# Payload and attribute rows in DRAM: from 16 and 132 bytes to 64 and 192 bytes

## The reference, cut to what matters

```python
def reference(x, src, dst, edge_attr_32, ...):
    edge_index = jnp.stack([src, dst])
    x = x + gnn(layernorm(x), edge_index, edge_attr_32, ...)     # relu(edge_attr @ W_time.T + b) summed over src
    x = x + moe6(layernorm(x), ...)                              # 6 experts of 3 layers, top 2
    x = x + gat2(layernorm(x), ..., src, dst)                    # 2 layers of graph attention, 256 channels
    x = x + routed_ffn(layernorm(x), ..., L1_ffn_edge_index)     # attention router over 131072 edges, 4 experts, top 2
    return x
```

## Time and profile before

| | |
|---|---|
| median of 3 runs | 10564.56 us (10502.92 to 10571.19) |
| the profiled execution | 10526.4 us |
| its span | 10524.6 us |
| TensorE's mean granted clock | 0.78 |
| busy: TensorE, VectorE, ScalarE, GpSimd | 53%, 52%, 34%, 55% |

### The profile page before, as it was taken

The page is one execution under the profiler, slowest core; times in us unless marked ns, Lnnn a source line. Parts: engine busy times, 40 slices in busy tenths (PEclk is TensorE's granted clock), DMA queues, the critical chain, the costliest instruction groups (busy, mean ns, idle before and its releaser), DMA issues. The chain is left out here.

```text
span 10524.6 us, 116781 instructions
## 1 busy us (share of the span) xinstructions
PE 5617.6 (53%) x22610; PEld 3283.4 (31%) x22610; DVE 5440.6 (52%) x18917; ACT 3525.9 (34%) x11436; POOL 5786.7 (55%) x5781
## 2 busy tenths in 40 slices
PE   0000001683321149936777764777772388888887
PEld 0000000571110025523444432444441134444444
DVE  8577300572200012235666654666664187777787
ACT  0000000230100012214555542555551076666662
POOL 3788767216577730045665654666666565565660
PEclk9999999995555579967777776777776577776678
DMA  4111100110000000003333321333330111111113
GB/s 126 24 21 22 24 9 4 27 33 2 2 23 1 1 1 0 0 22 85 88 86 85 87 63 55 86 86 87 88 87 15 23 20 23 22 23 23 23 23 99
DMA packets 476242, 426.24 MB, mean 40 GB/s; under 512 B 269726, under 2 KB 409876, under 8 KB 475668
## 3 DMA queue, kind: packets, MB, share of 16 engines
q0 software_dynamic: 214016, 282.62, 11.5%
q1 hardware_dynamic: 224020, 120.13, 4.2%
q10 hardware_dynamic: 37632, 17.48, 0.7%
HBM read 341.50 MB, written 78.72 MB: 40 GB/s over the span
## 5 line engine op out<-in xcount | busy, mean ns | idle before, releaser
L449 POOL DMA_INDIRECT pay_sorted<-pay,pos x1856 | 1880.9, 1013 | 1941.2 <-PEq L1217 762.7
L790 POOL DMA_INDIRECT G<-tab_gat,pay x1856 | 1783.6, 961 | 1314.1 <-issue 438.0
L790 POOL DMA_INDIRECT G<-tab_rt,pay x1216 | 1148.1, 944 | 822.0 <-PE pLU L867 346.1
L864 PE MATMUL pU<-G,PM 128*128 128x257 f32 x3712 | 1375.7, 505 | 0.8 <-DVE acc L1175 0.4
L274 POOL DMA_INDIRECT attr_sorted<-rows,pos x832 | 971.6, 1168 | 411.0 <-issue 253.1
L909 ACT ACTIVATE aT<-pA 20x256 bf16<-20x256 bf16 (+1 forms) x1232 | 522.2, 424 | 1457.6 <-PE pA L810 591.5
L864 PEld LDWEIGHTS pU<-G,PM 128*128 128x128 f32 x3712 | 809.7, 242 | 237.7 <-issue 87.3
L836 PE MATMUL pP<-ident,PT 128*128 128x128 f32 x1856 | 475.2, 347 | 764.7 <-ACT PM L961 640.3
L1679 DVE TENSOR_TENSOR t<-pO,BL 128x1024 f32<-128x1024 f32 (+1 forms) x78 | 90.7, 1163 | 1351.4 <-remote 714.0
L1078 DVE TENSOR_REDUCE mt<-pW 128x4 f32<-128x2048 f32 x304 | 695.1, 2286 | 155.0 <-PE pW L828 66.7
L1663 ACT ACTIVATE H<-pH,B 128x512 f32<-128x512 f32 (+1 forms) x312 | 206.3, 663 | 1370.9 <-remote 716.5
(11 more groups left out here) (324 smaller groups left out, 12068.8 us busy)
## 6 DMA issues: line engine op xcount, KB each, us to landing
pay_sorted<-pay,pos POOLq DMA_INDIRECT x1856
G<-tab_gat,pay POOLq DMA_INDIRECT x1856
G<-tab_rt,pay POOLq DMA_INDIRECT x1216
expert_parts<-pos SPq DMA_DIRECT2D x144, 128.0 KB
yl<-expert_parts SPq DMA_DIRECT2D x36, 512.0 KB, 4.0
attr_sorted<-zattr SPq DMA_DIRECT2D x1, 16896.0 KB, 53.1
rows<-attr_sorted ACTq DMA_DIRECT2D x256, 66.0 KB
attr_sorted<-rows,pos POOLq DMA_INDIRECT x832
```

What stands on the lines that cost most here:

```text
L449: pool.indirect_dma_start(out=out, out_offset=bass.IndirectOffsetOnAxis(ap=self.pos[g][:, lo + n:lo + n + 1], axis=0), in_=self.pay[g][:, ...
L790: pool.indirect_dma_start(out=G[:, j, k, 0:R], out_offset=None, in_=table, in_offset=bass.IndirectOffsetOnAxis(ap=pay[:, g % (2 * PART), k ...
L864: ins = nc.tensor.matmul(u[:, 0:F], PM[:, j % 2, k * P:(k + 1) * P], G[:, j, k, 0:F], start=(k == 0), stop=(k == K - 1))
```

## The change

The row pitches in DRAM become AW = 48 floats (192 bytes) for `attr_sorted` and DW = 16 words (64 bytes) for `pay_sorted`, and each scatter writes whole rows of that width. The source of a scattered row is the old column and what lies behind it in SBUF: for an attribute row 48 floats from column k's start, which take in 15 floats of the next column; for a payload row 16 words, its own 4 and the next three columns' 12. So the tiles get room at their ends: `room` (the old `rows`, 15 floats more for each chunk) and three more columns in `pay[g]`. What is read back is cut to the first 33 floats and the first 4 words of a row. The zero fills cover the wide rows. GpSimd has three memsets more (`room`, the tail of `zattr`, the tail of `zpay`), SyncE waits for four of `zattr` and not two, VectorE zeroes the three added columns of `pay[g]`, and the fills of `pay_sorted` move from SyncE's `fill` to the start of ScalarE's stream, on its own queue, behind a wait for `zpay`.

```diff
+AW = 48
+DW = 16
...
-        self.pay = [None, kp("pay1", [P, ET, PW], I32), kp("pay2", [P, FT, PW], I32)]
+        self.pay = [None, kp("pay1", [P, ET + DW // PW - 1, PW], I32), kp("pay2", [P, FT + DW // PW - 1, PW], I32)]
-        self.attr_sorted = nc.dram_tensor("attr_sorted", (NG0 * GE, ED + 1), F32).ap()
-        self.pay_sorted = [None] + [nc.dram_tensor(f"pay_sorted{g}", (NGS[g] * KS[g] * P, PW), I32).ap() for g in (1, 2)]
+        self.attr_sorted = nc.dram_tensor("attr_sorted", (NG0 * GE, AW), F32).ap()
+        self.pay_sorted = [None] + [nc.dram_tensor(f"pay_sorted{g}", (NGS[g] * KS[g] * P, DW), I32).ap() for g in (1, 2)]
...
-    def fill(self, sp, zpay, zrow, s_zpay):
+    def fill(self, sp, zrow, s_zpay):
...
-        sp.wait_ge(s_zpay, 5)
-        for dst in self.pay_sorted[1:]:
-            slots = dst.shape[0] // P
-            w = max(n for n in range(1, FILL + 1) if slots % n == 0)
-            loads.append(self.repeated(dst, zpay[:, 0:w, :].rearrange("p a b -> p (a b)")))
+        sp.wait_ge(s_zpay, 1)
...
-        return 16 * len(loads)
+        return 16 * (len(loads) + 2)
...
-            rows = sb("rows", [P, AR, AC, ED + 1])
+            room = sb("rows", [P, AR, AC * (ED + 1) + AW - ED - 1])
+            rows = room[:, :, 0:AC * (ED + 1)].rearrange("p a (b c) -> p a b c", b=AC)
-            zpay = sb("zpay", [P, FILL, PW], I32)
-            zattr, zrow = sb("zattr", [P, 8 * (ED + 1)]), sb("zrow", [1, D + 3])
+            zpay = sb("zpay", [P, FILL, DW], I32)
+            zattr, zrow = sb("zattr", [P, 8 * AW]), sb("zrow", [1, D + 3])
...
-                z3 = zattr[:, :].rearrange("p (r c) -> p r c", c=ED + 1)
+                z3 = zattr[:, :].rearrange("p (r c) -> p r c", c=AW)
+                pool.memset(room[:, :, :], 0.0).then_inc(s_zattr, 1)
                 pool.memset(z3[:, :, 0:ED], 0.0).then_inc(s_zattr, 1)
+                pool.memset(z3[:, :, ED + 1:AW], 0.0).then_inc(s_zattr, 1)
...
+                pool.memset(zpay[:, :, PW:DW], 0).then_inc(s_zpay, 1)
...
-                            in_=rows[:, j, k, :], in_offset=None,
+                            in_=room[:, j, k * (ED + 1):k * (ED + 1) + AW], in_offset=None,
...
-                sp.wait_ge(s_zattr, 2)
+                sp.wait_ge(s_zattr, 4)
...
             @block.scalar
             def _(act):
+                act.wait_ge(s_zpay, 6)
+                for dst in self.pay_sorted[1:]:
+                    slots = dst.shape[0] // P
+                    w = max(n for n in range(1, FILL + 1) if slots % n == 0)
+                    act.dma_start(*self.repeated(dst, zpay[:, 0:w, :].rearrange("p a b -> p (a b)"))).then_inc(self.s_x, 16)
                 act.wait_ge(s_lo0, 1)
...
+                        c(v.memset(self.pay[g][:, cc:, :], 0))
-                        c(v.tensor_copy(self.pay[g][:, :, 1].bitcast(F32), m2))
+                        c(v.tensor_copy(self.pay[g][:, 0:cc, 1].bitcast(F32), m2))
...
-        out = self.pay_sorted[g]
+        out, words = self.pay_sorted[g], self.pay[g][:, :, :].rearrange("p t w -> p (t w)")
...
-                in_=self.pay[g][:, lo + n, :], in_offset=None,
+                in_=words[:, (lo + n) * PW:(lo + n) * PW + DW], in_offset=None,
...
-            rows_v = self.attr_sorted.rearrange("(s p k) c -> p s k c", p=P, k=K)
+            rows_v = self.attr_sorted.rearrange("(s p k) c -> p s k c", p=P, k=K)[:, :, :, 0:ED + 1]
...
-            of = self.pay_sorted[gi].rearrange("(p s k) c -> p s k c", p=P, k=K)
+            of = self.pay_sorted[gi].rearrange("(p s k) c -> p s k c", p=P, k=K)[:, :, :, 0:PW]
```

More of the change, by code:

```diff
@@ L310, in _ @@
                     sp.dma_start(to, i["L1_ffn_edge_index"][r].rearrange("(p t) -> p t", p=P)).then_inc(s_key[2], 16)
-                filled = self.fill(sp, zpay, zrow, s_zpay)
+                filled = self.fill(sp, zrow, s_zpay)
                 for c in range(AR, NC):
@@ L421, in _ @@
                     if g:
+                        c(v.memset(self.pay[g][:, cc:, :], 0))
                         c(v.tensor_scalar(m2, kk, P - 1, None, ALU.bitwise_and))
-                        c(v.tensor_copy(self.pay[g][:, :, 1].bitcast(F32), m2))
+                        c(v.tensor_copy(self.pay[g][:, 0:cc, 1].bitcast(F32), m2))
                         src = key[:, 0, 0:cc] if g == 1 else oth[:, :]
-                        c(v.tensor_scalar(self.pay[g][:, :, 0], src, N - 1, None, ALU.min))
+                        c(v.tensor_scalar(self.pay[g][:, 0:cc, 0], src, N - 1, None, ALU.min))
                         for n in range(8):
                             c(v.tensor_scalar(kk, m2, n, 1, ALU.logical_shift_right, ALU.bitwise_and))
-                            c(v.tensor_copy(self.pay[g][:, :, 2:PW].bitcast(U8)[:, :, n], kk))
+                            c(v.tensor_copy(self.pay[g][:, 0:cc, 2:PW].bitcast(U8)[:, :, n], kk))
                 dve.wait_ge(self.s_x, 16 * 9)
```

## The result

The kernel before took 10502.38 us (median of 20 runs, 10465.14 to 10580.33), the changed one 10564.03 us (20 runs, 10493.37 to 10616.16). The ratio is 1.004, with a 95% interval of 1.002 to 1.0059. The forecast was 10585 us, +0.2%, in a range of 10470 to 10790. That the absolute time came out 21 us from the forecast is partly luck: the forecast started from 10564.56 us, the median of three runs, which the 20 runs put at 10502.38, and added 21 us where the medians differ by 62 (the means, 10515 and 10560, by 44, which is the ratio's 0.4%). The forecast's +21 us lies at the lower end of the interval. The profiled execution has a span of 10563.8 us against 10524.6.

A forecast was written before the change was run, and what follows sets the result against it. The prediction held that a delay of other engines under GpSimd's indirect DMAs, not arithmetic or bytes, takes most time in the edge and expert stages. Terms 2 + 2 + 17 = +21 us on 10564.56 gave 10585 us, range 10470 to 10790.

The forecast's parts named there:

- The scatters: GpSimd's payload and attribute scatters: same count and 1013 and 1168 ns each, 0 us, bounds -1350 to +0.
- the delay: Edge and expert stages: something holds back what other engines finish while GpSimd issues a scatter every 1.28 us.
- rival A: Edge, expert and smaller stages: the delay goes with full rows, -1350 us, to 9215 us; chance 0.20.
- the delay follows the rate of indirect DMAs: All stages with indirect DMAs: their rate, 128 rows each, sets the delay, not row content; the change leaves it alone.
- VectorE's recovery from 610 to 700 us: Sort stage: VectorE isn't held back because GpSimd issues one scatter per 1.76 us, against 1.40 in the slow stretch.
- Payload loads read back: Start of each attention: GpSimd waits longer for the first load, now in 16-byte pieces; +5, +5, +7 = +17 us.
- Rival B: Payload loads in all three attentions: small pieces slow them to 37 (49) us each, +120 to +250 us; chance 0.16.
- Attribute rows read back: Edge stage loads, 512 pieces of 132 bytes each: 0 us there, about 2 us at its start, bounds 0 to +40.
- Memsets: GpSimd's added memsets before VectorE's first sort: everything moves by +2 us, bounds 0 to 4.
- The fill: Zeroing DRAM, 42.7 MB in 125 us, covered by VectorE's first sort with 25 us left: 0 us.
- rival C: Zero fill before the first scatter: it outlasts its cover, +20 us; counted within the forecast, no chance of its own.
- The sum: Whole kernel: memsets 2, attribute read-back 2 and payload loads 17 make +21 us.

The follow-up runs named there:

- run 77: Not a run's label: "run" is a verb here, and 77 is the count of payload scatters that chips 6 and 10 do in 100 us.
- wider: The changed kernel with pitches doubled once more (attribute rows of 256 bytes, payload rows of 128): 10677.99 us beside 10612.77 for the kernel before, ratio 1.0063.

## Why the prediction was right, and where its working wasn't

- **The scatters.** "0 us", and it was: 1014 and 1160 ns each, the same windows. That the delay stays with rows of 64 and 192 bytes is shown, and it was the decision between the forecast and rival A (9215 us). The Trainium skill's rule in "Collectives: The Full Stack", section "Rules for kernel authors", that 32-byte alignment prevents a read-modify-write, brought nothing here that a run shows: the scatters' duration, and on chip 6 the time, are the same with rows of 16 and of 64 bytes.
- **The reason I gave for it.** "I take it that the delay follows the rate of indirect DMAs." It doesn't follow it alone: chips 6 and 10 run 77 payload scatters in 100 us, at the same 1.28 to 1.30 us each, without it (on chips 14 and 7 only spaced scatters were traced). My evidence was good against the rows' content (gathers of 1036 bytes showed the same dip) and I took it as evidence for a cause that it couldn't separate from the chip. The pace of the attentions' "steady part", a gather per 1.57 us (928 in 1453 us), isn't the kernel's own either: chip 6 has 928 in 1176. And VectorE's recovery from 610 to 700 us, read as the work of a lower rate, doesn't tell the rate from the chip.
- **Payload loads read back, +17 us.** Measured at GpSimd's wait: +4.1, +4.7, +5.6, 14.4 us; the price of a 16-byte piece, taken from the 128-byte pieces of the chunk load, was near. But I counted a wait as time. An attention that starts 4 to 6 us late ends 1 to 3 us late on chip 6. Rival B (37 to 49 us per load) is out.
- **Attribute rows read back, "0 us there".** This is the term that was mis-sized: ScalarE's issue grew from 0.34 to 0.55 us and the groups slowed by 3%, so the part of the edge stage behind the last scatter took 396 and not 387 us: +9, inside the bounds of 0 to +40. With the rows read whole both went back (0.34 us, 133 loads in 200 us), so it is the pieces; that they cost by ScalarE's issue and not by the queue's own time is how I read it, and no run holds the two apart. I had looked at the queue's use and the ring's depth, and not at the issue on ScalarE, which also does two activations for each group.
- **Memsets, +2 us.** The big one took 1.91 us, and the first scatter came 0.8 us later.
- **The fill.** Cover left was to be 25 us (to 164). The fill landed 120.0 us after its issue, at 126, and the loads behind it were issued at 130: some 30 us were left, and `wider` showed that beyond the cover it counts, rival C's mechanism.
- **The sum.** +21 us against +16 up to the third attention on one pair of executions, but not by the same terms: 16 us of it arise in the small stages between 2311 and 2943 us, under the delay, and on chip 6 those stages differ by under 1 us. On chip 6 the sum as a whole failed: +21 us would be a ratio of 1.0025 there, outside the interval. The step that doesn't hold there is the one from a wait to the total. Whether that is the change or the scatter of an execution can't be told from one trace of each; nor is it settled why the ratio is 1.004 where the delay exists and 0.9991 (0.9969 to 1.0013) where it doesn't. The 9 us of the edge stage are the only part of that difference that has been traced to a term.

## What to carry to other kernels

Cutting a DRAM row to what is needed on the way back trades bytes for pieces, and pieces were the dearer side twice: in the queue's time, and in the issue on the engine that starts the load. Widening and aligning rows that are written didn't move the scatter at all, so ask what a scatter's price hangs on before changing its rows; here it was GpSimd's issue, 1.3 us each, nearly all of it on the path on the chips without the delay. The dearer read-backs are seen in their own rows; in the whole time they are at most 0.4% on one chip and can't be told on another. And when a trace shows an effect that no row of the kernel explains, run the unchanged kernel on another chip before building a cause.

## What the runs showed that wasn't expected

The same program takes 10,500 to 10,600 us on two runs' chips and 8320 to 8350 us on four others. The difference lies where indirect DMAs and the other engines meet: in the kernel before the edge and expert stages take 897 and 1568 us on the first chip and 507 and 862 us on chip 6, the first attention's gathers 1453 and 1176 us, while what comes after the last gather takes 249 us on both. On a chip with the delay matmuls beside 128-row indirect DMAs fall to 32 to 43 in 100 us while GpSimd itself keeps its pace; the waits are for semaphores that come late, 22.8 us in the edge group shown. What makes them late, and what distinguishes the chips, isn't shown by any run here.
